# A two-layer graph transformer on one Trainium2 core: softmax scaling moved to GpSimd, the last norm's root made a power there, the projection's bias put into the folded weight, and the first gelu inside the loop

## The reference, cut to what matters

```python
xn = _layernorm(x)
x = x + _L1_gnn_ref(xn, U, s, Vt, bias, src, dst, edge_weight) + _L1_mix_ref(xn)
x = x + _L1_ffn_ref(_layernorm(x), fc1_w, fc1_b, fc2_w, fc2_b)

def _L1_mix_ref(x, w_qkv, w_proj, b_proj):          # 8 heads of 64
    q, k, v = ...
    q = softmax(q, axis=-1)                          # over the 64 values of a head
    k = softmax(elu(k) + 1.0, axis=-2)               # over the nodes
    context = einsum('bhnd,bhne->bhde', k, v)
    out = einsum('bhnd,bhde->bhne', q, context)      # then heads joined
    return out @ w_proj + b_proj

def _L1_ffn_ref(x, fc1_w, fc1_b, fc2_w, fc2_b):
    ll, lh, hl, hh = haar(x)                         # pairs of rows and columns
    h = gelu(interpolate(ll) @ fc1_w.T + fc1_b)
    return inverse_haar(h @ fc2_w.T + fc2_b, lh, hl, hh)
```

## Time and profile before

| | |
|---|---|
| time, median of 3 runs (lowest, highest) | 643.21 us (642.76, 645.39) |
| the profiled execution's own time | 646.26 us |
| its span in the profile | 644.5 us |
| PE busy | 580.7 us, 90% |
| DVE busy | 480.6 us, 75% |
| ACT busy | 323.1 us, 50% |
| POOL busy | 254.1 us, 39% |
| mean granted TensorE clock | 0.963 of full |

### The profile page before, as it was taken

One profiled execution on the slowest core, in us unless ns is written; L12 is line 12 of the kernel. 1 busy time (PEld: TensorE's weight loads), 2 busy tenths in 40 slices (PEclk: granted clock), 3 DMA queues, 4 the chain that ended last, 5 costly groups with the idle time before them and its releaser, 6 DMA issues.

```text
span 644.5 us, 8710 instructions
## 1 busy us (share of the span) xinstructions
PE 580.7 (90%) x2964; PEld 469.6 (73%) x2964; DVE 480.6 (75%) x1067; ACT 323.1 (50%) x612; POOL 254.1 (39%) x266
## 2 busy tenths in 40 slices
PE   3988899989999998999987999999979997998976
PEld 2776787767778676888765777877867886686866
DVE  7689988979997897688759766557665555677674
ACT  6767876867656721212135535334445774323161
POOL 4647666757787235356613900004010221022030
PEclk9999999999999898999999979899998998998989
DMA  9300000000010201022040100000020000110004
GB/s 318 118 2 1 1 1 2 2 1 1 2 65 3 66 16 33 18 75 34 14 138 1 67 0 1 1 1 1 1 81 2 1 1 1 39 45 0 1 2 159
DMA packets 15045, 21.11 MB, mean 33 GB/s; under 512 B 3260, under 2 KB 6000, under 8 KB 15002
## 3 DMA queue, kind: packets, MB, share of 16 engines
q1 hardware_dynamic: 13674, 17.94, 8.5%
q10 hardware_dynamic: 1328, 2.62, 1.2%
HBM read 18.00 MB, written 2.56 MB: 32 GB/s over the span
## 4 chain that ended last, share of the span: by engine, by line
PE 57%; DVE 23%; ACT 7%; issue 6%; POOL 4%; DVEq 1%; DMA 1%; SPq 1%; ACTq 0%; POOLq 0%
PE p L1975 6%; PE p L1825 4%; PE pQ L1841 4%; PE pQ L2089 3%; PE pH L1841 3%; PE p L2089 3%; DVE onehot L1240 3%; PE p L2202 2%; PE pQ L2264 2%; PE pH L1987 1%; POOL Loh L956 1%; PE p L1841 1%; PE pKV L1870 1%; PE pKV L2060 1%; PE p L2060 1%
## 5 line engine op out<-in xcount | busy, mean ns | idle before, releaser
L956 POOL TENSOR_TENSOR Loh<-onehot,whl 128x512 fp32r<-128x512 f32 x85 | 89.6, 1054 | 48.2 <-DVE onehot L1240 48.2
L1240 DVE TENSOR_SCALAR onehot<-iota_src,srclo 128x128 fp32r<-128x128 f32 x170 | 74.8, 480 | 0.7 <-DVE flagint L1252 0.7
L1975 PE MATMUL p<-G,ATs 128*128 128x512 f32 x300 | 70.8, 391 | 2.2 <-DVE G L1380 1.2
L1825 PEld LDWEIGHTS p<-Roh,Loh 128*128 128x128 f32 x340 | 48.3, 192 | 31.0 <-issue 27.0
L1975 PEld LDWEIGHTS p<-G,ATs 128*128 128x128 f32 x300 | 55.9, 188 | 14.8 <-issue 3.4
L1825 PE MATMUL p<-Roh,Loh 128*128 128x200 f32 x340 | 53.6, 280 | 11.6 <-POOL Loh L956 4.8
L559 ACT ACTIVATE away<-iota_key,key 128x200 f32<-128x200 f32 x85 | 38.7, 456 | 24.6 <-PE p L1825 24.6
L1841 PE MATMUL pQ<-wsl,xT 128*128 128x512 f32 x168 | 48.3, 417 | 2.3 <-DVE xT L1154 2.3
L1841 PE MATMUL pH<-wsl,xT 128*128 128x512 f32 x168 | 46.5, 405 | 0.0
L1091 POOL TENSOR_TENSOR xT<-xn,xT 128x512 fp32r<-128x512 f32 x10 | 12.9, 1293 | 74.6 <-ACT xT L778 74.2
L561 ACT ACTIVATE Roh<-away,onesf 128x200 fp32r<-128x200 f32 x85 | 39.3, 463 | 2.8
(11 more groups left out here) (584 smaller groups left out, 1484.5 us busy)
## 6 DMA issues: line engine op xcount, KB each, us to landing
xb<-in_x SPq DMA_DIRECT2D x9, 256.0 KB, 2.5
out<-nodes SPq DMA_DIRECT2D x9, 256.0 KB
wraw<-in_L_mix_w_qkv ACTq DMA_DIRECT2D x2, 1024.0 KB, 7.7
raw<-in_L_mix_w_qkv SPq DMA_DIRECT2D x2, 1024.0 KB, 5.1
nodes<-in_x SPq DMA_DIRECT2D x1, 1024.0 KB, 9.0
wraw<-in_L_mix_w_qkv SPq DMA_DIRECT2D x1, 1024.0 KB, 11.3
wraw<-in_L_gnn_W SPq DMA_DIRECT2D x1, 1024.0 KB, 13.5
raw<-in_L_mix_w_out SPq DMA_DIRECT2D x1, 1024.0 KB, 5.2
```

The lines of the kernel that those rows point to most:

```text
L956: pool.tensor_tensor(Loh[:, g % SLOTS], o, w, ALU.mult).then_inc(S["oh_pool"], 1)
L1240: ins = v.tensor_scalar(onehot_[:, g % SLOTS, c, :], iota_src[:], srclo[:, 2 * g + c:2 * g + c + 1], None, ALU.is_equal)
L1825: ins = pe.matmul(pW[g % 2][:, 0:T * WIN], Loh[:, g % SLOTS, c, part, :], Roh[:, g % RSLOTS, c, :], start=(c + part == 0), stop=(c + part ...
L1975: ins = pe.matmul(pG[u][:, :], ATs[:, u, x, s_, :], G[:, y, s_, :], start=(s_ + n == 0), stop=(s_ == T - 1 and n == 2))
```

## The change

It has five parts. (1) The ten softmax scalings leave DVE and stand on POOL: the first two right after the event that frees `et` and `rt`, the others behind the splitting of `PTh`. (2) The root and the reciprocal of the last norm become one power of -0.5 on POOL (`root`). (3) The projection's bias is divided by eight on DVE and added to each of the four `mw` blocks, since the eight softmaxes of a row sum to eight; the bias product in each `mix2` is gone. (4) Parts of the last norm stand one iteration later, and the first gelu stands inside ACT's loop at t = 8. (5) Behind the loop the orders of PE, DVE and ACT are changed.

```diff
@@ ACT @@
                 if t == 3:
                     act.wait_ge(S["w1_mm"], 1)
                     act.activation(W1[:, 0], ...).then_inc(S["w1_hi"], 1)
-                    ln_sqrt(7, *FOURS[0])
+                if t == 4:
                     sums_hi(0)
-                if t == 5:
+                if t == 6:
                     low_hi(0)
-                if t == 7:
-                    ln_sqrt(8, *FOURS[1])
+                if t == 8:
+                    gelu(0)
+                    doubled(0)
                     sums_hi(1)
             low_hi(1)
-            ln_sqrt(9, *FOURS[2])
-            gelu(0)
+            gelu(1)
             sums_hi(2)
-            gelu(1)
+            doubled(1)
             low_hi(2)
             gelu(2)
+            doubled(2)
@@ POOL @@
             pool.memset(b3[:].bitcast(F32), 0.0).then_inc(S["c1"], 1)
+            pool.wait_ge(S["zt_ps"], 1 + after["zt_ps"])
+            st(pool.memset(outside[:], -0.5))
+            for t in range(2):
+                o = (et, rt)[t][:].rearrange("p (h d) -> p h d", h=HEADS)
+                pool.tensor_tensor(o, qbuf[:, t, :]..., sumq[:, t, :]..., ALU.mult).then_inc(S["r2_qs"], 1)
             pool.wait_ge(S["ld_f1"], 64 + after["ld_f1"])
             for c in range(KC):
                 ins = pool.tensor_copy(PTh[:, 0, c], PTr[:, c])
...
+            def softmax(t):
+                if t >= 2:
+                    pool.wait_ge(S["r2_ps"], t - 1 + after["r2_ps"])
+                o = (et, rt)[t % 2][:].rearrange("p (h d) -> p h d", h=HEADS)
+                pool.tensor_tensor(o, qbuf[:, t, :]..., sumq[:, t, :]..., ALU.mult).then_inc(S["r2_qs"], 1)
+            def root(g):
+                t0, t1 = FOURS[g]
+                pool.wait_ge(S["ln_var"], 6 + g + 1)
+                pool.tensor_tensor(rstd[:, t0:t1], small[:, 3, t0:t1], outside..., ALU.pow).then_inc(S["ln_pow"], 1)
...
+            for t in range(2, 8):
+                softmax(t)
+            root(0)
+            scaled(0)
+            softmax(8)
+            softmax(9)
+            root(1)
+            scaled(1)
+            root(2)
+            scaled(2)
@@ DVE @@
-                v.wait_ge(S["ln_sqrt"], n)
-                step(v.reciprocal(r, r))
+                if n > 6:
+                    v.wait_ge(S["ln_pow"], n - 6 + after["ln_pow"])
...
-            softmax(0, 0, True)
             g2_lo(2)
-            softmax(1, 1, True)
             r2_lo(0, 0)
             v.wait_ge(S["ld_b2"], 32 + after["ld_b2"])
             v.wait_ge(S["c1"], 8)
+            step(v.tensor_scalar(xn[0:2, 1, :], xn[0:2, 1, :], 1.0 / HEADS, None, ALU.mult))
             step(v.tensor_copy(b2[0:2, :, :], xn[0:2, :, :]))
...
-                if t + 2 < T:
-                    softmax(t + 2, u)
                 total1(t, u)
...
+                if t == 4:
                     final_norm(0)
-                if t == 4:
+                    sums(0)
+                if t == 5:
                     sums_lo(0)
-                if t == 5:
+                if t == 6:
                     low_lo(0)
-                if t == 7:
+                if t == 8:
                     final_norm(1)
-                if t == 8:
-                    sums_lo(1)
+                    sums(1)
+                    gelu_lo(0)
+            sums_lo(1)
+            low_lo(1)
             final_norm(2)
-            low_lo(1)
-            gelu_lo(0)
+            sums(2)
+            result(0)
+            result(1)
             sums_lo(2)
...
@@ PE @@
-            pe.wait_ge(S["b2_ok"], 1)     # stood ahead of support(0, 0)
             for p, bank in enumerate(wbank2):
-                pe.matmul(bank[:, :], kT[:, p, :], Wp[:, p, :], start=True, stop=True).then_inc(S["mw_mm"], 1)
+                pe.matmul(bank[:, :], kT[:, p, :], Wp[:, p, :], start=True, stop=False)
+                if p == 0:
+                    pe.wait_ge(S["b2_ok"], 1)
+                pe.matmul(bank[:, :], rows1[:, 0, :], b2[:, 1, :], start=False, stop=True).then_inc(S["mw_mm"], 1)
...
-                pe.matmul(pM[u][:, :], rows1[:, 0, :], b2[:, 1, :], start=False, stop=True).then_inc(S["m2_mm"], 1)
+                ins.then_inc(S["m2_mm"], 1)
...
-                if t == 5:
+                if t == 6:
                     low(0)
                 if t == 7:
                     inner(0)
+            pe.wait_ge(S["b3_ok"], 1)
             low(1)
+            pe.wait_ge(S["x3_ok"], T + after["x3_ok"])
+            outer(0)
+            outer(1)
             inner(1)
-            pe.wait_ge(S["b3_ok"], 1)
-            pe.wait_ge(S["x3_ok"], T + after["x3_ok"])
-            for t in range(4):
-                outer(t)
+            outer(2)
+            outer(3)
             low(2)
```

More of the change, by code:

```diff
@@ L352, in build @@
                 ("ld_v1", "ld_w3", 16), ("ld_wp", "ld_wo", 16), ("ld_v2", "ld_x", 16), ("ld_b2", "b_ld", 32),
-                ("ld_f1", "ld_edge", 16 * 9)):
+                ("ld_f1", "ld_edge", 16 * 9), ("ln_pow", "pads_ok", 4)):
             S[name] = S[first_name]
@@ L877, in gelu, with doubled @@
                     act.activation(hf[:, b, r], hbank[g][:, b * HALF:b * HALF + n], ACT.Gelu, bias=fb1[:, b:b + 1]).then_inc(S["hh_g"], 1)
+            def doubled(g):
+                n = min(4, T - 4 * g) * DH
+                r = slice(4 * g * DH, 4 * g * DH + n)
                 act.wait_ge(S["hh_g"], 2 * g + 2)
@@ L1104, in _ @@
             pool.memset(b3[:].bitcast(F32), 0.0).then_inc(S["c1"], 1)
+            pool.wait_ge(S["zt_ps"], 1 + after["zt_ps"])
+            st(pool.memset(outside[:], -0.5))
+            for t in range(2):
+                o = (et, rt)[t][:].rearrange("p (h d) -> p h d", h=HEADS)
+                pool.tensor_tensor(o, qbuf[:, t, :].rearrange("p (h d) -> p h d", h=HEADS),
+                                   sumq[:, t, :].rearrange("p (h n) -> p h n", n=1).broadcast_to([P, HEADS, DH]), ALU.mult).then_inc(S["r2_qs"], 1)
             pool.wait_ge(S["ld_f1"], 64 + after["ld_f1"])
@@ L1112, in _, with scaled @@
             ins.then_inc(S["pt_lo"], 1)
-            for g, (t0, t1) in enumerate(FOURS):
+            def softmax(t):
+                if t >= 2:
+                    pool.wait_ge(S["r2_ps"], t - 1 + after["r2_ps"])
+                o = (et, rt)[t % 2][:].rearrange("p (h d) -> p h d", h=HEADS)
+                pool.tensor_tensor(o, qbuf[:, t, :].rearrange("p (h d) -> p h d", h=HEADS),
+                                   sumq[:, t, :].rearrange("p (h n) -> p h n", n=1).broadcast_to([P, HEADS, DH]), ALU.mult).then_inc(S["r2_qs"], 1)
+            def root(g):
+                t0, t1 = FOURS[g]
+                pool.wait_ge(S["ln_var"], 6 + g + 1)
+                pool.tensor_tensor(rstd[:, t0:t1], small[:, 3, t0:t1], outside[:, 0:1].broadcast_to([P, t1 - t0]), ALU.pow).then_inc(S["ln_pow"], 1)
+            def scaled(g):
+                t0, t1 = FOURS[g]
                 pool.wait_ge(S["s_add"], g + 1)
@@ L1145, in ln_coefficients @@
                 v.tensor_scalar(var, mv[:, t0:t1, 1], EPS, None, ALU.add).then_inc(S["ln_var"], 1)
-                v.wait_ge(S["ln_sqrt"], n)
-                step(v.reciprocal(r, r))
+                if n > 6:
+                    v.wait_ge(S["ln_pow"], n - 6 + after["ln_pow"])
+                else:
+                    v.wait_ge(S["ln_sqrt"], n)
+                    step(v.reciprocal(r, r))
                 newton(var, r, small[:, 2, t0:t1])
@@ L1679, in _ @@
                 a2_lo(k)
[L1681 to L1685, removed]
             def r2_lo(t, u):
@@ L1721, in final_norm, with sums @@
                 step(v.tensor_scalar(nmr2[:, t0:t1], nmr[:, t0:t1], 2.0, None, ALU.mult))
+            def sums(g):
+                t0, t1 = FOURS[g]
                 x2v = nodes[:, t0:t1, :].rearrange("p t (i v) -> p t i v", v=2)
@@ L1776, in _ @@
                     v.tensor_tensor(W1[:, 1], pKV[0][:, :].rearrange("p (c n) -> p c n", c=2), W1[:, 0].bitcast(F32), ALU.subtract).then_inc(S["w1_lo"], 1)
+                if t == 4:
                     final_norm(0)
-                if t == 4:
+                    sums(0)
+                if t == 5:
                     sums_lo(0)
-                if t == 5:
+                if t == 6:
                     low_lo(0)
-                if t == 7:
+                if t == 8:
                     final_norm(1)
-                if t == 8:
-                    sums_lo(1)
+                    sums(1)
+                    gelu_lo(0)
+            sums_lo(1)
+            low_lo(1)
             final_norm(2)
-            low_lo(1)
-            gelu_lo(0)
+            sums(2)
+            result(0)
+            result(1)
             sums_lo(2)
-            for t in range(4):
-                result(t)
             gelu_lo(1)
+            result(2)
+            result(3)
             low_lo(2)
-            for t in range(4, 8):
+            for t in range(4, 7):
                 result(t)
             gelu_lo(2)
-            for t in range(8, T):
```

(5 more changed lines are left out.)

## The result

The changed kernel is slower: 655.85 us (median of 4 runs, 655.12 to 656.32) against 643.33 for the kernel before; the ratio is 1.0185, 95% interval 1.0165 to 1.0205. That is 12.5 us more where 5.9 had been forecast. The direction was right, the forecast was half of the size, and the time lies outside the range given (up to 653.5).

The account below looks back on a forecast made before the run. PE's feeding bounds the kernel, each hole of about 3 us costing 1.6 more in clock. 9.8 - 0.7 + 1.6 - 4.3 - 0.5 = +5.9 us on the median 643.21 gives 649.1, own range 646.5 to 652.5 (wider: 645.8 to 653.5).

Parts of the forecast that it names:

- The queue on POOL: Ahead of turn2(2): softmax(2) waits on POOL behind load and split of PTh, so turn2(2) starts 9.8 us late, fold's delay included.
- The fold: Folded weight ahead of the loop: PE waits for b2_ok, so the four blocks are ready 3.1 us late.
- The long hole: PE idles 7.4 us ahead of turn2(2); the lower clock behind it costs 1.6 us.
- The hole at the norm: First group's norm in the loop: PE's hole of 2.94 us becomes 1.2, too short for the clock to fall.
- p: Time of the norm's power on POOL, taken as 0.5 us, between 0.20 and 3.1.
- The tail: Behind mix2(8): a new 6 us hole ahead of low(1), won back by the earlier gelu; end at 32.2 us, -0.5.
- B: Rival, GpSimd is dearer: power 3.1 us, clock after the long hole 1.6 more; half of this 654, all 658; chance 0.13.
- a power over 1 us: Sign in the changed kernel's profile, at the norms on POOL, that would speak for rival B.
- A: Rival, the loop pays more back: quicker load and split, tail at its lower end; +3.0, 646.2 us; chance 0.12.
- C: Rival, faster: turn2(2) is not held by POOL, the 7.4 us hole and its 1.6 go; 640.1 us; chance 0.04.
- The tenths that the two early scalings were expected to lose: POOL's two early scalings beside DVE's splits of ZT: contention at SBUF would cost some tenths of a us.

Follow-up runs that it names:

- Run 4: Changed kernel with the softmax scalings of tiles 2 and 3 ahead of the split of PTh on POOL; 646.81 us, ratio 1.0048.
- run 3: Changed kernel with the bias rows b2 prepared earlier in DVE's idle time, products and bias rows still in turn; 651.94 us, ratio 1.014.
- run 8: Kernel of run 6 with the roots of groups 0 and 1 back on ACT, reciprocal on DVE; 639.97 us, ratio 0.9933.
- Run 9: Changed kernel with 26 unread 128x512 products added on PE ahead of low(1); 652.35 us, ratio 1.0131.
- run 2: Changed kernel with the four folding products first, then the wait for b2_ok and the four bias products; 650.8 us, ratio 1.011.
- run 6: Changed kernel with b2 early, scalings of tiles 2 and 3 ahead of PTh's split, group 1's norm and first gelu at t = 7; 638.01 us.
- run 10: Kernel of run 6 with seven unread products added on PE ahead of low(1); 635.85 us, ratio 0.987.
- Run 7: Kernel before with only the softmax scaling moved to GpSimd, tiles 0 to 3 ahead of the split of PTh; 643.15 us, ratio 0.9976.

## Why the prediction was half right

**The queue on POOL: right.** The load, the split and the scaling come one after the other, and `turn2(2)` is released by POOL: forecast +6.7 between the load's issue and `turn2(2)`, measured +6.5. POOL starts 6.83 us after the issue (6.41 forecast), the split is shorter (4.25 for 4.66), the scaling takes 1.04 for 1.29. Run 4 shows that this order alone is worth 9 us.

**The fold: the mechanism right, its size wrong.** This is the step that failed first: "From 559.75: 0.23, then three pairs of 0.9 + 0.23", prices at full clock. `b2_ok` came where forecast, 3.0 after F. The prediction had read from its rows that PE's holes cost clock, and did not apply it to the hole that it had itself worked out, since it priced only holes of about 3 us. The first bias row and the three pairs ran at half clock for most of their time: 3.0 us more (run 3 has the same rows without the hole, at full clock).

**The long hole: right.** 1.6 was charged; the twelve products took 4.61 for 2.98, and the transposes ahead of them 0.4 more: 2.0 in all.

**The hole at the norm: the power's price.** Forecast 1.2 with p = 0.5, measured 1.61 with p = 1.05. "Nearer to the row of the same size" was the wrong choice: a power and a subtraction of the same 128x4 took 1.05 and 0.20. A second small loss was not foreseen: DVE's low part of the sums took 1.94 us beside POOL's scalings, where it takes 1.23 alone, and `low(0)` waited 0.26 for it. That the clock stays up here was called a choice, and it came out so; with 1.97 in place of 1.61 (run 8) it didn't.

**The tail: wrong.** Forecast -0.5, measured +3.0. The hole was forecast at 6 us and is 6.64; what failed is "`low(1)` takes from 1.97 to 3.4" as the only place that pays. The clock stayed down for 8 us, from 629.3 to about 637.5: `low(1)`, both outer products and the first half of `inner(1)`. Run 9 takes the low clock away and gives back 3.5 us. Of these the forecast had charged 1.4 (3.4 less 1.97), so 2.1 of the error were the clock. The rest, 1.4 us, was not: `low(1)` starts 10.44 us after `mix2(8)`, not 10, and some 0.9 behind it were not traced. That run 9's tail, 32.0 us, is nearly the 32.2 of the forecast is luck, for the forecast has the 1.4 in it.

**The rivals.** B had the right sign and nearly the size, and by the prediction's own sign, a power over 1 us, it is in part what happened. But the power was 1.05, not 3.1. Over the price taken it cost 0.55, 0.51 and 0.20 in the three groups; 1.3 in all is an estimate, if all three lie on the path. The clock after the long hole cost 0.4 more than charged, not 1.6. A and C did not happen. With the clock's 3.0 in the fold and 2.1 in the tail the forecast's sum would have been 11.0 us; the medians say 12.5, the two traces 13.4. The power would bring it near the medians; no run shows that sum. The tenths that the two early scalings were expected to lose did not come: they took 1.04 us each, and DVE's splits of `ZT` beside them 1.29 for two and 0.68, as before. Those splits read one of their two inputs from a bank of PE, not from SBUF.

## What to carry to other kernels

A wait on TensorE has two prices: the idle time and the half clock behind it. Work out both cases for every hole that the change makes, the one of 2 us too (here 1.9 to 2.0 us was followed by half clock, 1.6 was not), and follow the second through all that stands behind it. When an instruction moves to another engine's queue, read what it lands behind there before its duration: here its place was worth 9 us, while its duration was hidden in all tiles but one. An early wait for a small preparation can be answered by making the preparation earlier, in idle DVE time (run 3), or by putting what needs it behind the other products (run 2); the two measured 651.9 and 650.8 us, with intervals that overlap.

## What the runs showed of the hardware

- Holes of 1.92 us (fold), 1.90 (run 6) and 1.97 (the norm in run 8) were followed within 1 us by the clock's lower level; holes of 1.61 (the norm), 1.32 (ahead of `low(2)`, run 10) and 1.15 (there, changed kernel and run 8) were not. But length alone doesn't decide. In run 6 the clock fell 2.1 us after a hole of 1.16 at that same place, and in the kernel before it stayed up for 0.9 us after a hole of 3.00 (PE starts again at 542.77) and then fell. What decides is open.
- The lower level lasted 8 us behind the hole of 6.64 in the changed kernel although PE was busy throughout, and 6 us behind the one of 1.92 in the fold; behind the same 1.92 in run 4 it lasted 3.4 us.
- Filling holes with unread products gained 3.5 us in run 9 and, less surely, about 2 in run 10.
- A power on GpSimd took 1.05 and 1.01 us for 128x4 and 0.70 for 128x2, where a `TENSOR_TENSOR` of 128x4 takes 0.20.
- DVE and GpSimd, each with two SBUF inputs, held each other up. In the changed kernel's timeline:

```profile
606.09 1.04 POOL L1129 TENSOR_TENSOR et<-qbuf,sumq 128x512 f32<-128x512 f32 x1
...
606.27 1.94 DVE L1763 TENSOR_TENSOR shl<-sn,shl 128x1024 fp32r<-128x1024 f32 x1 [0.66 <-ACT shl L864]
...
607.09 2.02 POOL L1129 TENSOR_TENSOR rt<-qbuf,sumq 128x512 f32<-128x512 f32 x1
```

  Alone DVE's takes 1.23 and POOL's 1.04. The three end at 607.13, 608.21 and 609.11, some 1.0 us apart: what started first lost nothing, and each of the others took about as long as if it had begun when the one ahead ended. Run 7 has the same (1.95 and 2.02). The GPSIMD Engine Reference of the Trainium skill (section 8) says that the two contend at their SBUF interfaces where DVE's instruction has two SBUF inputs; the trace agrees.
- Products of f32 and of fp32r in turn cost nothing beside their own time (run 3: 1.09 us a pair).
